# Weight maxima turned by TensorE, the last 42 MLP rows stacked, and sums of rotated terms moved to VectorE

## The chip, the cores and the metric

One core of one Trainium2 chip. The metric is the device time of one execution in microseconds, as the median of several runs. Lower is better.

## The reference, cut to what matters

The input is x of 4 x 2048 x 256 in float32. Every step works on the layer norm of what came before, and its own layer norm is added to x.

```python
x = x + layernorm(self_attention(layernorm(x)))      # scores x @ x.T, softmax over axis 1, whole sequence
y = layernorm(x)
for l in range(2):                                   # DEPTH = 2
    q, k, v = split(shift_token(y) @ wqkv[l])        # 8 heads of 64
    q, k = l2norm(q) * q_scale, l2norm(k) * k_scale  # then rotated: t * cos + rotate_half(t) * sin
    y = y + local_attention(q, k, v) @ wo[l]         # windows of 128, each with the window before it
    h = layernorm(shift_token(y)) * ln_g[l] + ln_b[l]
    a, g = split(h @ w1[l] + b1[l])                  # HID = 682 each = 5 * 128 + 42
    y = y + (a * gelu(g)) @ w2[l] + b2[l]
out = x + layernorm(y)
```

## The kernel before, in words

The work is cut in windows of 128 rows: 64 of them (4 sequences of 16), and as each passes two layers, 128 steps in the second part. Five queues run side by side and meet at semaphores: SP issues all DMAs, PE is TensorE, DVE is VectorE, ACT is ScalarE, POOL is GpSimd. Each engine does its instructions strictly in the order written; an order across engines exists only where one waits.

**Phase A** is the attention over whole sequences. For each sequence TensorE makes 16 blocks of scores, then 16 windows of context, called products (line 657): 48 matmuls of 256 columns per window, into PSUM banks 0 to 3 in turn. VectorE closes each window in finish(g) (lines 512 to 546): statistics of the product (L519 to L523), normalising it (L529), adding the input (L533, x_res, loaded two windows ahead), statistics of the sum (L535 to L539), normalising that (L546). It needs two inverse roots in between, and both come from GpSimd: rstd_c (L349, L351) before L529 and rstd_x (L355) before L546. SP stores both results. TensorE may be at most three windows ahead of L529.

In the last sequence, the scratch memory of the scores is free again, and the weights of the MLP are loaded there by early_weights() (lines 257 to 268: w1, w2, then wo). They must be scaled by powers of two before they are split in two float16 halves. For this, VectorE takes maxima of |w2| in windows 4 and 5 and of |w1| in windows 6 to 9 (L465, L471); tops(), after window 10, brings them to one value per partition for three quantities and two layers, and a square for each layer (L477 to L483). share_tops() on GpSimd, after window 10, takes the maximum over the 128 partitions of the six columns and the sum over the partitions of the two squares, with two partition_all_reduce (L319, L321). scales(), on VectorE after window 13, waits for both and makes the factors, 15 small instructions in a chain (L488 to L510).

**Phase B** begins behind a barrier of all engines. Weights are split in halves by ScalarE (L779 to L789) and VectorE (L794 to L813), and then a software pipeline runs over 128 slots (plus 6 to drain). In slot s:
- TensorE turns q and k of window s-1 (L994, L1001), projects window s (L1016, 18 matmuls of 512 columns), turns the probabilities of s-2 (L1032), multiplies them with v (L1044), makes the scores of s-1 (L1057), multiplies the attention's output of s-2 with wo (L1070), and turns the input of s+1 (L983). In an even slot it then makes the first product of the MLP for a pair of windows (L1091, 66 matmuls), in an odd slot the second (L1103).
- ScalarE squares q and k for the norms, copies from PSUM, and does the exponentials and the gelu.
- VectorE makes the two terms of the rotation of q and k (L1216, L1217: t1 and t2), sums the squares (L1224), adds the context in an odd slot of layer 1 (L1266, fin + x2), takes the low half of the attention output (L1271), reduces eight heads of scores (L1303), then the residual (L1324), normalises probabilities (L1315, eight times), takes the low half of the next input (L1203) and, in an even slot, finishes the MLP's hidden chunks (L1337, six of them).
- GpSimd halves the squares (L1380), in an odd slot splits hidden chunks 4 and 5 in halves (L1352, L1354; chunks 0 to 3 at the end of an even slot), adds t1 and t2 for q (L1388, qr) and for k (L1390, kr_sum), clamps the sums of squares (L1394), takes the inverse root for k (L1396), multiplies k with it (L1400, kr), and takes the inverse root for q (L1404). TensorE's L994 needs qr and its L1001 needs kr.

Products of float32 accuracy are made of high and low halves: PARTS = ((0, 0), (0, 1), (1, 0)) is high by high, high by low, low by high. L1103 runs over n in 2 windows, 6 chunks of the hidden rows and these three parts, 36 matmuls of 256 columns; chunk 5 (FULL) holds 42 rows (REST), the other partitions being zero.

## Time and profile before

| | |
|---|---|
| median of 3 runs | 3042.15 us (3039.99 to 3045.44) |
| the profiled execution's own time | 3045.73 us |
| its span, first to last instruction | 3043.9 us |
| TensorE | 2896.4 us busy, 95%, 25720 matmuls, clock granted 0.982 of full on average |
| VectorE | 2421.9 us, 80% |
| ScalarE | 2044.8 us, 67% |
| GpSimd | 2045.6 us, 67% |
| DMA | 179.01 MB, mean 59 GB/s |

All numbers below are from this one profiled execution, and so are to be set against 3045.73 us. A timeline row gives the start and the length of an instruction (or of a run of equal ones, with their count), the engine, the line of the kernel, what is written and what is read, and in brackets how long the engine was idle just before and what ended that. Lengths of neighbours on VectorE overlap by some 0.1 us, so that the distance of starts is the better price. Phase A and its load of weights take up to about 691 us; the stream of phase B begins at about 713 us.

### The profile page before, as it was taken

The page shows a single profiled execution, that of the slowest core. Times are in us where ns is not written, and L with a number is a line of the kernel's source. Part 1 is how long each engine was busy: PE and PEld are TensorE (multiplying, and loading weights), DVE is VectorE, ACT ScalarE, POOL GpSimd, SP SyncE. Part 2 cuts the span into 40 slices and gives each one's busy share as a digit, 9 for nine tenths or more (in the row PEclk, how much of TensorE's full clock was granted, in tenths as well). Part 3 has the DMA queues.
Part 4 walks back from the last instruction along what each step waited for, and adds up shares of the span by engine and source line. Part 5 has one row for each costly group of instructions (what it writes and reads, how often), then busy time and mean ns, then how long its engine had stood idle before and what let it go on. Part 6 is the DMA issues. An engine that isn't in the chain of part 4 may idle for free. (4 is left out here: it accounts for less than half of the span.)

```text
span 3043.9 us, 81674 instructions
## 1 busy us (share of the span) xinstructions
PE 2896.4 (95%) x25720; PEld 2508.8 (82%) x25720; DVE 2421.9 (80%) x6767; ACT 2044.8 (67%) x4648; POOL 2045.6 (67%) x2782
## 2 busy tenths in 40 slices
PE   7899999984999999999999999999999999999996
PEld 4767777773888888888888888888888888888885
DVE  7779898756778778777777877788888888888884
ACT  6234343504777777777777777777788787778874
POOL 0432323014777777777777777888888888888884
PEclk9999999987999999999999999999999999999998
DMA  1421212212111121111111111122222112222221
GB/s 40 143 83 39 74 35 70 91 55 75 53 50 50 52 58 50 54 50 48 51 54 55 50 55 50 50 59 61 66 57 62 55 55 59 64 61 59 60 53 44
DMA packets 274932, 179.01 MB, mean 59 GB/s; under 512 B 96014, under 2 KB 271090, under 8 KB 274802
## 3 DMA queue, kind: packets, MB, share of 16 engines
q1 hardware_dynamic: 274802, 177.34, 20.1%
q8 instruction: 75, 1.23, 0.2%
q14 instruction: 55, 0.45, 0.1%
HBM read 105.92 MB, written 54.54 MB: 53 GB/s over the span
## 5 line engine op out<-in xcount | busy, mean ns | idle before, releaser
L1177 ACT ACTIVATE b_front<-b_front,b_negmax 128x256 f32<-128x256 f32 x1024 | 507.8, 497 | 77.2 <-DVE b_negmax L1303 76.4
L1016 PE MATMUL b_ps<-b_wqkv,b_hT_hi 128*128 128x512 f32 x1536 | 497.1, 405 | 2.6 <-issue 1.5
L1091 PE MATMUL b_ps<-b_h2T,b_w 128*128 128x256 f16 x4224 | 474.2, 273 | 9.2 <-DMA b_h2T<-b_xh_hl 9.2
L1091 PEld LDWEIGHTS b_ps<-b_h2T,b_w 128*128 128x128 f16 x4224 | 414.2, 98 | 58.3 <-DMA b_h2T<-b_xh_hl 8.8
L1315 DVE TENSOR_SCALAR b_front<-b_front,b_rinv 128x256 f32<-128x256 f32 x1024 | 338.4, 393 | 9.1
L1016 PEld LDWEIGHTS b_ps<-b_wqkv,b_hT_hi 128*128 128x128 f32 x1536 | 283.1, 191 | 61.4 <-issue 2.2
L1303 DVE CUSTOM_DVE_ANT_0 b_front<-b_ps,b_mask,b_rn 128x256 f32<-128x256 f32 x768 | 317.7, 479 | 0.0
L1159 ACT COPY b_front<-b_ps 128x512 f32<-128x512 f32 x512 | 260.8, 593 | 80.3 <-PE b_ps L1032 80.3
L1016 PE MATMUL b_ps<-b_wqkv,b_hT_lo 128*128 128x512 f32 x768 | 305.9, 398 | 0.0
L1271 DVE TENSOR_TENSOR b_oT<-b_ps,b_oT 128x512 fp32r<-128x512 f32 x128 | 88.6, 692 | 262.6 <-ACT b_oT L1168 262.6
L1354 POOL TENSOR_TENSOR b_hid_hl<-b_front,b_hid_hl 128x256 f16<-128x256 f32 (+1 forms) x384 | 258.7, 674 | 31.0
L1103 PE MATMUL b_ps<-b_w,b_hid_hl 128*128 128x256 f16 x2304 | 264.8, 274 | 3.3 <-POOL b_hid_hl L1354 3.3
L1044 PE MATMUL b_ps<-b_front 128*64 128x128 f32 x4096 | 253.0, 276 | 0.9 <-ACT b_front L1159 0.9
L1103 PEld LDWEIGHTS b_ps<-b_w,b_hid_hl 128*128 128x128 f16 x2304 | 226.5, 98 | 30.4 <-POOL b_hid_hl L1354 3.6
L1032 PEld LDWEIGHTS b_ps<-b_ident_f,b_front 128*128 128x128 f32 x2048 | 232.1, 141 | 22.0 <-DVE b_xpp L1247 3.3
L1032 PE MATMUL b_ps<-b_ident_f,b_front 128*128 128x128 f32 x2048 | 245.4, 273 | 4.3 <-DVE b_xpp L1247 3.1
L1044 PEld LDWEIGHTS b_ps<-b_front 128*64 128x64 f32 x4096 | 221.5, 137 | 23.5 <-issue 13.5
L1352 POOL CAST b_hid_hl<-b_front 128x256 f16<-128x256 f32 (+1 forms) x384 | 165.2, 430 | 111.2 <-DVE b_front L1337 92.8
L1192 ACT ACTIVATE b_gl<-b_ps,b_b,b_w_unit 128x256 f32<-128x256 f32 (+1 forms) x384 | 202.9, 561 | 54.7 <-PE b_ps L1091 32.4
L1337 DVE SCALAR_TENSOR_TENSOR b_front<-b_ps,b_b1a,b_gl 128x256 f32<-128x256 f32 (+1 forms) x384 | 177.4, 480 | 62.8 <-ACT b_gl L1192 60.9
L1404 POOL TENSOR_TENSOR b_rn<-b_ss_min,b_mhalf 128x8 f32<-128x8 f32 x128 | 223.4, 1745 | 0.0
L1396 POOL TENSOR_TENSOR b_rn_k<-b_ss_min,b_mhalf 128x8 f32<-128x8 f32 x128 | 214.0, 1672 | 10.7
(171 smaller groups left out, 7076.0 us busy)
## 6 DMA issues: line engine op xcount, KB each, us to landing
b_hx<-xs_dram SPq DMA_DIRECT2D x256, 64.0 KB, 1.9
b_rot<-rot_dram SPq DMA_DIRECT2D x128, 128.0 KB, 2.1
b_xr<-xs_dram SPq DMA_DIRECT2D x128, 128.0 KB, 2.1
xp_dram<-b_xp SPq DMA_DIRECT2D x128, 128.0 KB, 1.7
b_h<-xp_dram SPq DMA_DIRECT2D x256, 64.0 KB, 1.8
a_x_res<-in_L_attn_x_dram SPq DMA_DIRECT2D x64, 128.0 KB, 2.2
x_dram<-a_x SPq DMA_DIRECT2D x64, 128.0 KB, 1.7
xs_dram<-a_xo SPq DMA_DIRECT2D x64, 128.0 KB, 1.8
```

The source lines that it names most:

```text
L1016: last = nc.tensor.matmul(ps[:, bank, :], hT[:, k, :], wqkv[:, ds(layer(s), 1), part, k, bank * INNER:(bank + 1) * INNER], start=(k == 0 a ...
L1032: last = nc.tensor.transpose(ps[:, 3 + p, n * P:(n + 1) * P], probs[:, 2 * p + n // 2, (n % 2) * P:(n % 2 + 1) * P], ident_f[:])
L1044: last = nc.tensor.matmul(ps[h * DH:(h + 1) * DH, 7, p * P:(p + 1) * P], v[:, window, (2 * p + h) * DH:(2 * p + h + 1) * DH], probsT[:, p, ...
L1091: last = nc.tensor.matmul(ps[:, bank, half * 2 * P:(half + 1) * 2 * P], w1[:, ds(layer(2 * j), 1), wp, k, first:first + P], h2T[:, hp, k, ...
L1103: last = nc.tensor.matmul(ps[:, 3, n * D:(n + 1) * D], hid_hl[:, hp, c, n * P:(n + 1) * P], w2[:, ds(layer(2 * j), 1), wp, c, :], start=(c ...
L1159: nc.scalar.copy(probsT[:, p, :], ps[:, 3 + p, :]).then_inc(pT_kept, 1)
L1177: nc.scalar.activation(probs[:, h, :], probs[:, h, :], ACT.Exp, bias=negmax[:, h:h + 1], scale=-1.0, accum_out=rowsum[:, h:h + 1]).then_in ...
L1303: nc.vector.tensor_tensor_reduce(probs[:, h, :], head_scores(h), which, rn[:, (r - 1) % 2, h:h + 1], ABOVE_ALL, ALU.add, ALU.min, negmax[: ...
L1315: nc.vector.tensor_scalar(probs[:, h, :], probs[:, h, :], rinv[:, h:h + 1], None, ALU.mult).then_inc(probs_ready, 1)
L1354: nc.gpsimd.tensor_tensor(hid_hl[rows, 1, c, :], hid[rows, c, :], hid_hl[rows, 0, c, :], ALU.subtract).then_inc(hid_lo, 1)
L1396: nc.gpsimd.tensor_tensor(rn_k[:], ss_min[:, HEADS:2 * HEADS], mhalf[:, 0:HEADS], ALU.pow).then_inc(rnk_ready, 1)
L1404: nc.gpsimd.tensor_tensor(rn[:, r % 2, :], ss_min[:, 0:HEADS], mhalf[:, 0:HEADS], ALU.pow).then_inc(rn_ready, 1)
```

## The change

1. share_tops() leaves GpSimd. tops() stays after window 10. TensorE turns the six columns after product 12 (turn_tops, into PSUM bank 7), VectorE reduces them over the columns to six values and spreads these on a diagonal after window 12 (highest_tops), and TensorE multiplies a matrix of ones with the diagonal and with the squares after product 14 (share_tops, bank 6). scales() moves from after window 13 to after window 14, and begins with two copies out of PSUM. GpSimd clears a 128x128 matrix of ones at the start.
2. Chunk 5 of the hidden rows: its low half is written to partitions 64 to 105 of the high half's tile, w2's last 42 rows are loaded twice (partitions 0 to 41 and 64 to 105), and L1103 makes two parts instead of three there. GpSimd waits for its last write of a pair. The loads of w2 and wo count on one semaphore, and the maxima of w2 wait for all six.
3. A function sum_terms on VectorE stands between sum_squares and add_context. It makes k's sum of t1 and t2 in odd slots, and q's and k's in slots 0 to 3 (filling(s) is true there alone). GpSimd makes the others: q's from slot 4 on, k's in even slots from 4 on.

```diff
+REST_PARTS = ((0, 0), (0, 1))
-W2_MAXIMA_AT, W1_MAXIMA_AT, SHARE_AT, SCALES_AT = 4, 6, 10, 13
+W2_MAXIMA_AT, W1_MAXIMA_AT, TOPS_AT, TURN_AT, SCALES_AT = 4, 6, 10, 12, 14
...
@@ early_weights(), SP @@
-                sp.dma_start(early.w2_f[0:REST, :, FULL, :], w["w2"][:, FULL * P:HID, :].rearrange("l p d -> p l d")).then_inc(early.loaded_w2, 16)
+                for first_row in (0, SECOND_REST):
+                    sp.dma_start(early.w2_f[first_row:first_row + REST, :, FULL, :], w["w2"][:, FULL * P:HID, :].rearrange("l p d -> p l d")).then_inc(early.loaded_w2, 16)
...
@@ phase A, POOL @@
+            nc.gpsimd.memset(ones[:], 1.0).then_inc(pool_consts, 1)
...
-            def share_tops():
-                pool.wait_ge(early.top_ready, 3)
-                nc.gpsimd.partition_all_reduce(early.top_all[:].rearrange("p n l -> p (n l)"), early.top[:].rearrange("p n l -> p (n l)"), P,
-                                               RED_MAX).then_inc(early.top_shared, 1)
-                nc.gpsimd.partition_all_reduce(early.sq_all[:], early.top_sq[:], P, RED_ADD).then_inc(early.top_shared, 1)
...
-                    if g == NW - WPB + SHARE_AT:
-                        share_tops()
...
@@ weight_maximum(), DVE @@
-                    dve.wait_ge(early.loaded_w2, 16 * 3)
+                    dve.wait_ge(early.loaded_w2, 16 * (4 + LAYERS))
...
+            def highest_tops():
+
+                dve.wait_ge(early.top_turned, 1)
+                nc.vector.tensor_reduce(highest[:], ps[0:by_weight, 7, 0:P], AX.X, ALU.max).then_inc(early.tops, 1)
+                dve.wait_ge(early.tops, 3)
+                nc.vector.tensor_scalar(spread[:], ident_f[0:by_weight, 0:by_weight], highest[:], None, ALU.mult).then_inc(early.top_ready, 1)
...
             def scales():
                 dve.wait_ge(early.top_shared, 2)
+                nc.vector.tensor_copy(top_all[:].rearrange("p n l -> p (n l)"), ps[:, 6, 0:by_weight]).then_inc(early.tops, 1)
+                nc.vector.tensor_copy(early.sq_all[:], ps[:, 6, by_weight:by_weight + LAYERS]).then_inc(early.tops, 1)
+                dve.wait_ge(early.tops, 5)
...
@@ phase A, PE @@
+                def turn_tops():
+
+                    pe.wait_ge(early.top_ready, 3)
+                    nc.tensor.transpose(ps[0:by_weight, 7, 0:P], early.top[:].rearrange("p n l -> p (n l)"), ident_f[:]).then_inc(early.top_turned, 1)
+
+                def share_tops():
+
+                    pe.wait_ge(pool_consts, 2)
+                    pe.wait_ge(early.top_ready, 4)
+                    nc.tensor.matmul(ps[:, 6, 0:by_weight], ones[0:by_weight, :], spread[:], start=True, stop=True).then_inc(early.top_shared, 1)
+                    nc.tensor.matmul(ps[:, 6, by_weight:by_weight + LAYERS], ones[:], early.top_sq[:], start=True, stop=True).then_inc(early.top_shared, 1)
...
@@ phase B, L1103, PE @@
-                                for a, (hp, wp) in enumerate(PARTS):
+                                for a, (hp, wp) in enumerate(PARTS if c < FULL else REST_PARTS):
...
@@ phase B, DVE @@
+                def sum_terms(s, r):
+
+                    if filling(s):
+                        dve.wait_ge(q_terms, 2 * (s + 1))
+                        wait(dve, qT_done, s)
+                        nc.vector.tensor_tensor(qr[:], t1[:, 0, :], t2[:, 0, :], ALU.add).then_inc(qr_ready, 1)
+                    if in_range(s) and (filling(s) or r % 2 == 1):
+                        dve.wait_ge(k_terms, 2 * (s + 1))
+                        nc.vector.tensor_tensor(t1[:, 1, :], t1[:, 1, :], t2[:, 1, :], ALU.add).then_inc(kr_sum, 1)
...
                     sum_squares(s)
+                    sum_terms(s, r)
                     add_context(pairs - 3, r, layer)
...
@@ phase B, hid_halves(), POOL @@
-                            nc.gpsimd.tensor_tensor(hid_hl[rows, 1, c, :], hid[rows, c, :], hid_hl[rows, 0, c, :], ALU.subtract).then_inc(hid_lo, 1)
+                            low = hid_hl[rows, 1, c, :] if c < FULL else hid_hl[SECOND_REST:SECOND_REST + REST, 0, c, :]
+                            nc.gpsimd.tensor_tensor(low, hid[rows, c, :], hid_hl[rows, 0, c, :], ALU.subtract).then_inc(hid_lo, 1)
+                            if c == FULL:
+                                pool.wait_ge(hid_lo, HC * (j + 1))
...
@@ phase B, run(), POOL @@
-                    if in_range(s):
+                    if in_range(s) and not filling(s):
                         pool.wait_ge(q_terms, 2 * (s + 1))
                         wait(pool, qT_done, s)
                         nc.gpsimd.tensor_tensor(qr[:], t1[:, 0, :], t2[:, 0, :], ALU.add).then_inc(qr_ready, 1)
+                    if in_range(s) and not filling(s) and r % 2 == 0:
                         pool.wait_ge(k_terms, 2 * (s + 1))
                         nc.gpsimd.tensor_tensor(t1[:, 1, :], t1[:, 1, :], t2[:, 1, :], ALU.add).then_inc(kr_sum, 1)
```

## Rows read from the trace of the kernel before

**Rows 1.** Busy us (x count) by stretch: PE, PEld, DVE, ACT, POOL, clock, DMA
```profile
900.00:1500.00 600.00, 600.00 (x5525) 535.81 (x5523) 473.16 (x1422) 458.70 (x1120) 474.31 (x621) 1.00 0.18 52
...
2000.00:2500.00 500.00, 499.48 (x4591) 445.60 (x4589) 425.50 (x1252) 398.39 (x959) 429.55 (x573) 1.00 0.21 60
```
**Rows 2.** PE timeline, seam: start, length, what, xcount, [idle before <-what ended it]
```profile
624.78 46.56 PE L657 MATMUL a_ps<-a_xn_odd,a_E 128*128 128x256 f16 x425
```
**Rows 3.** Timeline of DVE at the seam
```profile
645.17 0.43 DVE L519 BATCH_NORM_STATS2 a_st_c<-a_ps 128x6 f32<-128x256 f32 x1 [0.50 <-PE a_ps L657]
...
650.41 0.43 DVE L519 BATCH_NORM_STATS2 a_st_c<-a_ps 128x6 f32<-128x256 f32 x1
...
664.57 0.54 DVE L529 TENSOR_SCALAR a_ln_c<-a_ps,a_mv_c,a_rstd_c 128x256 f32<-128x256 f32 x1 [13.32 <-POOL a_rstd_c L351]
...
676.68 0.15 DVE L488 TENSOR_TENSOR b_bias_sq<-b_top_all 128x2 f32<-128x2 f32 x1
...
678.69 0.16 DVE L510 TENSOR_TENSOR b_w_unit<-b_w1a_unit,b_w_low 128x2 f32<-128x2 f32 x1
...
683.39 0.42 DVE L519 BATCH_NORM_STATS2 a_st_c<-a_ps 128x6 f32<-128x256 f32 x1
...
687.68 0.42 DVE L546 TENSOR_SCALAR a_xo<-a_x,a_mv_x,a_rstd_x 128x256 f32<-128x256 f32 x1 [0.66 <-POOL a_rstd_x L355]
```
**Rows 4.** Timeline of POOL at the seam
```profile
655.22 0.40 POOL L319 PARTITION_ALL_REDUCE b_top_all<-b_top  x1 [5.80 <-issue]
...
663.68 0.59 POOL L349 TENSOR_TENSOR a_pow_c<-a_var_c,a_mhalf 128x1 f32<-128x1 f32 x1 [7.67 <-issue]
```
**Rows 5.** Timeline of PE in the first slots of phase B
```profile
730.58 1.11 PE L1001 MATMUL b_ps<-b_ident_f,b_kr 128*128 128x128 f32 x4 [3.85 <-POOL b_kr L1400]
...
743.89 1.17 PE L1016 MATMUL b_ps<-b_wqkv,b_hT_hi 128*128 128x512 f32 x2
```
**Rows 6.** Timeline of PE in the stream, layer 0, then layer 1
```profile
1233.54 4.09 PE L1103 MATMUL b_ps<-b_w,b_hid_hl 128*128 128x256 f16 x36
...
1237.47 0.60 PE L994 MATMUL b_ps<-b_ident_f,b_front 128*128 128x128 f32 x4
...
2225.00 1.69 PE L1070 MATMUL b_ps<-b_wo,b_oT 128*128 128x256 f32 x12
```
**Rows 7.** Timeline of POOL in slots 0 and 1
```profile
725.98 1.26 POOL L1390 TENSOR_TENSOR b_front<-b_front 128x512 f32<-128x512 f32 x1
...
729.48 1.04 POOL L1400 TENSOR_TENSOR b_kr<-b_front,b_rn_k 128x512 f32<-128x512 f32 x1
...
742.00 1.04 POOL L1400 TENSOR_TENSOR b_kr<-b_front,b_rn_k 128x512 f32<-128x512 f32 x1
```
**Rows 8.** DVE timeline, an odd slot of layer 0, then of layer 1
```profile
1230.93 0.69 DVE L1271 TENSOR_TENSOR b_oT<-b_ps,b_oT 128x512 fp32r<-128x512 f32 x1 [2.65 <-ACT b_oT L1168]
...
2221.36 1.00 DVE L1266 TENSOR_TENSOR b_fin<-b_fin,b_x 128x512 f32<-128x512 f32 x1
...
2224.13 0.69 DVE L1271 TENSOR_TENSOR b_oT<-b_ps,b_oT 128x512 fp32r<-128x512 f32 x1 [1.76 <-ACT b_oT L1168]
```
**Rows 9.** The line L1266: ns min/median/max, first and last start
```profile
L1266 DVE TENSOR_TENSOR b_fin<-b_fin,b_x x32: 693/1006/1197, 1972.6 to 3040.4; 128x512 f32<-128x512 f32 x32
```
**Rows 10.** Timeline of DVE in slots 1 and 2
```profile
741.52 1.93 DVE L1315 TENSOR_SCALAR b_front<-b_front,b_rinv 128x256 f32<-128x256 f32 x4
...
743.37 0.41 DVE L1203 TENSOR_TENSOR b_hT_lo<-b_ps,b_hT_hi 128x256 fp32r<-128x256 f32 x1
...
743.90 1.14 DVE L1315 TENSOR_SCALAR b_front<-b_front,b_rinv 128x256 f32<-128x256 f32 x4
...
754.18 0.69 DVE L1271 TENSOR_TENSOR b_oT<-b_ps,b_oT 128x512 fp32r<-128x512 f32 x1 [2.98 <-ACT b_oT L1168]
```
**Rows 11.** Timeline of SP, the issue of the last w2 load
```profile
585.48 0.92 SPq L266 DMA_DIRECT2D b_front<-in_L_ffn_w_dram  x1
```
**Rows 12.** Timeline of DVE, window 6 of the last batch
```profile
624.21 0.43 DVE L519 BATCH_NORM_STATS2 a_st_c<-a_ps 128x6 f32<-128x256 f32 x1 [8.55 <-PE a_ps L657]
```

More of the change, by code:

```diff
@@ L126, in __init__ @@
         self.w1_unit, self.w2_unit = sb("w1_unit", [P, LAYERS]), sb("w2_unit", [P, LAYERS])
-        self.cleared, self.loaded_bias, self.loaded_w2, self.loaded_wo = (sem(n) for n in (
-            "cleared", "loaded_bias", "loaded_w2", "loaded_wo"))
+        self.cleared, self.loaded_bias, self.loaded_w2 = (sem(n) for n in (
+            "cleared", "loaded_bias", "loaded_w2"))
         self.loaded_w1 = [sem(f"loaded_w1_{l}") for l in range(LAYERS)]
-        self.bias_done, self.w1_gained, self.maxima, self.tops, self.top_ready, self.top_shared = (sem(n) for n in (
-            "bias_done", "w1_gained", "maxima", "tops", "top_ready", "top_shared"))
+        self.bias_done, self.w1_gained, self.maxima, self.tops, self.top_ready, self.top_shared, self.top_turned = (sem(n) for n in (
+            "bias_done", "w1_gained", "maxima", "tops", "top_ready", "top_shared", "top_turned"))
         self.step, self.scale_ready = sem("step"), sem("scale_ready")
@@ L179, in phase_a @@
         zeros = sb("zeros", [LAYERS * B, D])
+        ones = sb("ones", [P, P])
+        by_weight = 3 * LAYERS
+        highest, spread = sb("highest", [by_weight, 1]), sb("spread", [by_weight, by_weight])
         ps = ctx.enter_context(nc.psum_tensor("a_ps", [P, 8, 512], F32))
@@ L220, in _ @@
                 sp.dma_start(x_ring[:, n % ring, :], x_v[:, n, :]).then_inc(ring_in[n % ring], 16)
-            sp.wait_ge(pool_consts, 1)
+            sp.wait_ge(pool_consts, 2)
             rows = BLOCKS_PER_BATCH * P
@@ L556, in _ @@
                     finish(g)
-                    if g == NW - WPB + SHARE_AT:
+                    if g == NW - WPB + TOPS_AT:
                         tops()
+                    if g == NW - WPB + TURN_AT:
+                        highest_tops()
                     if g == NW - WPB + SCALES_AT:
@@ L690, in _ @@
                         biases(i - W2_MAXIMA_AT)
+                    elif i == TURN_AT:
+                        turn_tops()
+                    elif i == SCALES_AT:
+                        share_tops()
                 if b < B - 1:
@@ L697, in in_range, with filling @@
     return not isinstance(t, int) or 0 <= t < NT
+def filling(s):
+    return isinstance(s, int) and s < SLOTS
 def slots(eng, run):
@@ L776, in _ @@
             def _(act):
-                act.wait_ge(early.loaded_wo, 16 * LAYERS)
+                act.wait_ge(early.loaded_w2, 16 * (4 + LAYERS))
                 for l in range(LAYERS):
@@ L1101, in run @@
                             for c in range(HC):
-                                for a, (hp, wp) in enumerate(PARTS):
+                                for a, (hp, wp) in enumerate(PARTS if c < FULL else REST_PARTS):
                                     last = nc.tensor.matmul(ps[:, 3, n * D:(n + 1) * D], hid_hl[:, hp, c, n * P:(n + 1) * P],
                                                             w2[:, ds(layer(2 * j), 1), wp, c, :],
-                                                            start=(c == 0 and a == 0), stop=(c == HC - 1 and a == 2))
+                                                            start=(c == 0 and a == 0), stop=(c == HC - 1 and a == 1))
                         last.then_inc(w2_done, 1)
@@ L1432, in _ @@
                 nc.gpsimd.memset(kT_low[:].bitcast(F32), 0.0).then_inc(vk_cleared, 1)
-                nc.gpsimd.memset(hid_hl[:, :, FULL, :], 0.0).then_inc(vk_cleared, 1)
+                nc.gpsimd.memset(hid_hl[:, 0, FULL, :], 0.0).then_inc(vk_cleared, 1)
                 slots(pool, run)
```

4 lines of the change are left out of this document (2 added, 2 removed).

## The prediction

> **What bounds the kernel now.** I read the busy time by stretches first [rows 1]. In the stream of slots that fills the last three quarters of the span, TensorE is busy for 600.00 of 600 us in one stretch and 499.48 of 500 in the other, at the full clock; VectorE and GpSimd have some 15 to 20% free. There a microsecond off TensorE's queue is a microsecond off the end, and one moved between VectorE and GpSimd is worth nothing unless it makes TensorE wait. The seam between the phases is another matter: TensorE does its last product of phase A at 624.78 + 46.56 = 671.34 [rows 2], but VectorE closes the last window only at 687.68 + 0.42 = 688.10 [rows 3], and phase B waits for that. So at the seam VectorE's chain is the path, and it was held: L529 stood 13.32 us for GpSimd [rows 3], whose queue had the two all-reduces of share_tops ahead of that window's root, with 5.80 and 7.67 us of idle around them [rows 4]. The 0.40 us shown for an all-reduce is no measure of it, the 13.32 is. Last, in the first slots of phase B TensorE waits for GpSimd's k, 3.85 us at L1001 [rows 5].
>
> **The change, part by part.**
>
> (a) The seam. Two all-reduces leave GpSimd. TensorE gains a transpose after product 12 and two matmuls of 6 and 2 columns after product 14; VectorE gains a reduction and a 6x6 scaling after window 12, and two small copies ahead of the scale chain, which moves from behind window 13 to behind window 14. Without the stall each window is closed as its product comes: products come 650.41 - 645.17 = 5.24 us apart, closing one takes 683.39 to 688.10, 4.71 us [rows 3]. Window 11 starts at 650.41 as before, 12 at 655.65, closed at 660.36. Now the reduction and the scaling: the transpose they wait for is in TensorE's queue at 655.65 and done by 656. I give both, with their waits, 0.55 us (small instructions here take 0.15, and the 15 of the scale chain, many of which wait for the one before, run from 676.68 to 678.85 [rows 3]); they end at 660.9. Window 13 starts at 655.65 + 5.24 + 0.3 = 661.2, so they are hidden; the 0.3 is the transpose, as four of 128x128 took 1.11 us after an idle [rows 5]. Window 14 starts at 666.4 and is closed at 671.1. TensorE's two matmuls stand at 666.4 and want VectorE's 660.9: 5.5 us of room. Then the scale chain, 678.69 + 0.16 - 676.68 = 2.17 us, with two copies and a wait, 0.4: 673.7. Window 15, its product done by 671.9, ends at 673.7 + 4.71 = 678.4. Against 688.10 that is **-9.7 us**. Bounds: with all seven new instructions free, 650.41 + 3 x 5.24 + 4.71 + 2.17 + 4.71 = 677.7, -10.4; with 0.15 us more for each, -8.6. All of phase B starts behind this barrier and shifts with it.
>
> (b) The sixth chunk of the MLP's second product. Per pair of windows 36 matmuls of 256 columns become 34. The 36 take from 1233.54 to 1237.47, 3.93 us, 0.109 each [rows 6]. 64 pairs make 128 fewer: **-13.9 us**. Bounds: -13.5 if the last two pairs, where TensorE may wait anyway, give nothing; -14.2 if one is spared at half the clock. GpSimd's last subtraction writes other partitions at its old size, and GpSimd then waits for its own write, some 0.1 us per pair. Queued behind that wait are q's sum and the norms; k's own sum leaves that queue, so all of it still ends earlier than now.
>
> (c) Odd slots, k's sum on VectorE. GpSimd loses one instruction of 1.26 us [rows 7] in each of 64 slots; VectorE gains one of about 0.69, the length of L1271, which also has 512 columns [rows 8]. It stands after the sum of squares and ahead of L1271, before which VectorE idles 2.65 us in layer 0 and 1.76 in layer 1 [rows 8]. So it costs nothing, and the relief of GpSimd brings nothing, as TensorE waits for neither. Layer 1 needs a closer look, as L1266 stands in the same gap and reads both operands from the same memory, as the new sum does. L1266 takes 1.006 us by the median and 0.693 at least [rows 9]: beside a busy GpSimd such an instruction is held up. I give the sum L1266's place and length, 2221.36 to 2222.36, and L1266 another 1.0 behind it, to 2223.4. ScalarE's input for L1271 comes at 2224.13 [rows 8], 0.7 later. Still nothing, with less room. Without that cover each 0.1 us would count, as L1271 ends at 2224.82 and TensorE's L1070, which needs it, starts at 2225.00 [rows 6].
> The Trainium skill (SBUF — State Buffer, "Who interferes with whom") has a rule for this: a VectorE instruction with two inputs in SBUF and a GpSimd instruction that reads SBUF exclude each other, and the later one waits for the whole of the earlier. The spread of L1266 from 0.693 to 1.197 us agrees. By it the sum could stand behind a whole GpSimd sum, and the rival below comes of that; GpSimd would be held as well.
>
> (d) Slots 0 to 3, both sums on VectorE. In slot 0 two sums of 1.26 us leave GpSimd's queue between the halving and the norms. VectorE's sum of squares, also over 512 columns, is ready a 0.69 and a wait after the halving, some 0.8 us, so the norms start 2 x 1.26 - 0.8 = 1.7 us earlier, and k is out 1.7 us before its 729.48 + 1.04 = 730.52 [rows 7]; 0.8 if VectorE's sums and the norms' first steps hold each other up. In slot 1 VectorE is the path: L1203 ends at 743.37 + 0.41 = 743.78 [rows 10] and TensorE's projections start at 743.89 [rows 5]. The new sums put 2 x 0.6 us ahead of it. Against that VectorE starts 0.8 to 1.7 earlier, and four L1315 that took 1.93 us beside GpSimd's L1400 at 742.00 [rows 7, 10] take 1.14, as the next four do, once L1400 is done earlier. Middle of the bounds: -1.25 - 0.8 + 1.2, **-0.9 us**, from -0.4 to -1.3. In slots 2 and 3 the 1.2 us fall into an idle of 2.98 before L1271 [rows 10]: nothing. The outermost bounds are -1.7 (only k's chain counts) and +1.2 (only VectorE's queue).
>
> (e) Costed at nothing: one more load for w2, 84 KB. SP's issue of the one like it took 0.92 us [rows 11], so the loads, stores and residual rows behind it come up to that much later, and so does the closing of window 3; VectorE's 8.55 us of idle at 624.21 [rows 12] cover it, without them it would be 0.9. W2's maxima now wait for wo's loads too, in front of the same cover. The memset of the ones stands where GpSimd waits for the first rows.
>
> **Sum.** -9.7 - 13.9 - 0.9 = -24.5 us. The profiled execution took 3045.73 us (3043.9 of span and 1.8 around it); one like it would take 3021.2. It lies 3.6 above the median of the three runs, 3042.15; from the median the sum gives 3017.7.
>
> **Rivals.**
> The two engines lock each other out (slower). In layer 1's odd slots L1266 loses to GpSimd's last subtraction and then to q's sum of 1.26 us as well, and ends some 1.8 us later than I gave, at 2225.2. L1271 then starts 1.07 late, and TensorE at L1070 with it. 29 slots (the 32 of L1266 less three after the last projections) by 1.07 is +31: 3048.7. It decides once L1266 ends past 2224.13. For it: the mere 0.2 us of room between L1271 and L1070. Against: L1266 never took over 1.197 us [rows 9]. 0.04.
> The shorter product is absorbed. TensorE is at the next slot 0.22 us sooner and waits there for VectorE's L1203 or GpSimd's k. Then (b) gives nothing: 3031.6. Against: TensorE has no idle in 600 us [rows 1]. 0.07.
> The seam gives half: TensorE's in-order queue stands at one of its two new waits, or the barrier is held by something that the stall hid. 3022.6. The 5.5 us of room speak against it. 0.08.
> The edits do not do what they say, or two of these together: 3036 and above. 0.03.
>
> **How the numbers follow.** The forecast keeps 0.78; its own range, with its bounds and the 3 us by which runs of a kernel lie from the median, is 3012 to 3023. To hold 8 in 10 with something for what no row shows, I go on to the second rival: 3010 to 3031. A measurement can tell some 0.2%, 6 us, from no change. Faster 0.78 + 0.07 + 0.08 = 0.93, within 0.2% 0.03, slower 0.04.
>
> **What would show it.** (a) No wait of L529 over 1 us; the last window closed near 678.4. (b) L1103 x2176, 34 matmuls in 3.71 us, two slots 0.22 us shorter. (c) VectorE's sum 0.7 us long, up to 1.2 beside GpSimd; L1070 with no idle. (d) k 0.8 to 1.7 us earlier in slot 0, slot 2's projections 0.9 earlier, both counted from the barrier. The prediction would be wrong if TensorE showed waits at L1070 in layer 1, or if the time from its last product of phase A to its first work in phase B stayed what it was.

## The result, and the profile after

| | before | changed |
|---|---|---|
| median of the runs on one chip | 3043.80 us (3039.99 to 3046.31) | **3021.36 us** (3019.62 to 3025.50) |
| ratio, 95% interval | | **0.9929** [0.9915, 0.9942] |
| profiled execution, span | 3043.9 us | 3023.7 us |

The kernel is 0.7% faster, 22.4 us by the medians and 20.2 by the spans of the two profiled executions. First the page's busy times, as in the table ahead of the prediction.

```profile
PE 2887.6 (95%) x25597; PEld 2497.1 (83%) x25597; DVE 2466.3 (82%) x6841; ACT 2043.6 (68%) x4648; POOL 1978.3 (65%) x2711
```

GpSimd has lost 67 us of work (2045.6 before), VectorE has gained 44. Of each, what matters is where. In the rows that follow, lines have moved: L519, L529, L546 and L657 of phase A are L527, L537, L554 and L667 now, and L994, L1016, L1032, L1070, L1103, L1266 and L1271 of phase B are L1025, L1047, L1063, L1101, L1134, L1307 and L1312.

**The seam**, from the timeline of all engines, against [rows 3]:

```profile
655.77 0.27 PE L685 MATMUL a_ps<-a_ident_f,b_top 128*6 128x128 f32 x1
...
657.73 0.54 DVE L537 TENSOR_SCALAR a_ln_c<-a_ps,a_mv_c,a_rstd_c 128x256 f32<-128x256 f32 x1 [0.92 <-POOL a_rstd_c L351]
...
660.59 0.27 DVE L486 TENSOR_REDUCE a_highest<-a_ps 6x1 f32<-6x128 f32 x1
660.89 0.22 DVE L488 TENSOR_SCALAR a_spread<-a_ident_f,a_highest 6x6 f32<-6x6 f32 x1
661.33 0.43 DVE L527 BATCH_NORM_STATS2 a_st_c<-a_ps 128x6 f32<-128x256 f32 x1 [0.21 <-PE a_ps L667]
...
666.46 0.38 PE L691 MATMUL a_ps<-a_spread,a_ones 6*128 6x6 f32 x2
...
671.18 0.16 DVE L493 COPY b_top_all<-a_ps 128x6 f32<-128x6 f32 x1
...
673.53 0.42 DVE L527 BATCH_NORM_STATS2 a_st_c<-a_ps 128x6 f32<-128x256 f32 x1
...
677.81 0.41 DVE L554 TENSOR_SCALAR a_xo<-a_x,a_mv_x,a_rstd_x 128x256 f32<-128x256 f32 x1 [0.66 <-POOL a_rstd_x L355]
...
681.11 0.37 DVE L825 TENSOR_SCALAR b_b1a<-b_b,b_w1a_scale 128x6 f32<-128x6 f32 x2 [2.89 <-PEq L149]
```

The wait of 13.32 us before L529 is 0.92 now, as for every other window. TensorE's ones product stands 5.4 us behind the 6x6 scaling that it needs and waits for nothing. The last window is closed at 677.81 + 0.41 = 678.22, where it was 688.10, and phase B's first work after the barrier starts at 681.11, 9.87 us sooner than before:

```profile
690.98 0.36 DVE L794 TENSOR_SCALAR b_b1a<-b_b,b_w1a_scale 128x6 f32<-128x6 f32 x2 [2.88 <-PEq L148]
```

**The stream.** One pair of slots takes 35.253 us where it took 35.420. This is the distance from the first L1134 of one pair to that of the next, as a mean of 24 pairs in the steady part of a layer, which is 12 rounds of the loop of four slots; both layers give the same. That is 0.167 less, not the 0.218 that two matmuls cost. The timeline of TensorE after, layer 0, and under it the same two steps before:

```profile
1220.79 3.88 PE L1134 MATMUL b_ps<-b_w,b_hid_hl 128*128 128x256 f16 x34
1224.50 0.60 PE L1025 MATMUL b_ps<-b_ident_f,b_front 128*128 128x128 f32 x4
...
1225.29 0.71 PE L1047 MATMUL b_ps<-b_wqkv,b_hT_hi 128*128 128x512 f32 x2
...
1229.58 1.91 PE L1063 MATMUL b_ps<-b_ident_f,b_front 128*128 128x128 f32 x16
```

```profile
1238.26 0.71 PE L1016 MATMUL b_ps<-b_wqkv,b_hT_hi 128*128 128x512 f32 x2
...
1242.52 1.91 PE L1032 MATMUL b_ps<-b_ident_f,b_front 128*128 128x128 f32 x16
```

The 34 matmuls take 1224.50 - 1220.79 = 3.71 us, as forecast. But the 18 projection matmuls of a slot, between the first L1047 and L1063, take 4.29 us where they took 4.26; in the steady part of layer 0 it is 4.289 in every slot, against 4.264 in even and 4.275 in odd ones. Nothing in the change touches them. With some 0.01 us elsewhere that is 0.05 us per pair taken back.

**The odd slot of layer 1**, where the lock was feared [rows 8], from the timeline after:

```profile
2204.59 1.01 DVE L1259 TENSOR_TENSOR b_front<-b_front 128x512 f32<-128x512 f32 x1
2205.52 0.88 DVE L1307 TENSOR_TENSOR b_fin<-b_fin,b_x 128x512 f32<-128x512 f32 x1
...
2205.93 0.99 POOL L1397 TENSOR_TENSOR b_hid_hl<-b_front,b_hid_hl 42x256 f16<-42x256 f32 x1
...
2207.15 1.29 POOL L1433 TENSOR_TENSOR b_front<-b_front 128x512 f32<-128x512 f32 x1 [0.23 <-POOL b_hid_hl L1397]
...
2207.36 0.69 DVE L1312 TENSOR_TENSOR b_oT<-b_ps,b_oT 128x512 fp32r<-128x512 f32 x1 [0.96 <-ACT b_oT L1199]
...
2208.22 1.69 PE L1101 MATMUL b_ps<-b_wo,b_oT 128*128 128x256 f32 x12
```

The new sum takes 1.01 us, L1307 0.88 behind it, and L1312 still waits 0.96 us for ScalarE: TensorE's L1101 loses nothing. GpSimd's last subtraction pays, 0.99 us for 0.67, and its wait for its own write costs it 0.23 more.

### The profile page after: what moved, and what is told of

It is laid out like the page before. It is cut to its first block and busy times, and to the rows that moved or that the text cites. A ratio compares the mean times of both kernels' runs of the same rounds, so it can differ in the third digit from the quotient of the medians.

```text
span 3023.7 us, 81512 instructions
## 1 busy us (share of the span) xinstructions
PE 2887.6 (95%) x25597; PEld 2497.1 (83%) x25597; DVE 2466.3 (82%) x6841; ACT 2043.6 (68%) x4648; POOL 1978.3 (65%) x2711
## 3 DMA queue, kind: packets, MB, share of 16 engines
q1 hardware_dynamic: 274900, 177.42, 20.2%
## 5 line engine op out<-in xcount | busy, mean ns | idle before, releaser
L1047 PE MATMUL b_ps<-b_wqkv,b_hT_hi 128*128 128x512 f32 x1536 | 497.9, 405 | 2.9 <-issue 1.9
L1047 PEld LDWEIGHTS b_ps<-b_wqkv,b_hT_hi 128*128 128x128 f32 x1536 | 282.6, 191 | 63.4 <-issue 2.7
L1357 DVE TENSOR_SCALAR b_front<-b_front,b_rinv 128x256 f32<-128x256 f32 x1024 | 324.4, 379 | 9.0
L1047 PE MATMUL b_ps<-b_wqkv,b_hT_lo 128*128 128x512 f32 x768 | 306.9, 400 | 0.0
L1397 POOL TENSOR_TENSOR b_hid_hl<-b_front,b_hid_hl 128x256 f16<-128x256 f32 (+1 forms) x384 | 268.7, 700 | 31.0
L1312 DVE TENSOR_TENSOR b_oT<-b_ps,b_oT 128x512 fp32r<-128x512 f32 x128 | 88.5, 691 | 208.1 <-ACT b_oT L1199 208.1
L1394 POOL CAST b_hid_hl<-b_front 128x256 f16<-128x256 f32 (+1 forms) x384 | 180.9, 471 | 114.5 <-DVE b_front L1379 95.5
L1134 PE MATMUL b_ps<-b_w,b_hid_hl 128*128 128x256 f16 x2176 | 250.9, 274 | 3.3 <-POOL b_hid_hl L1397 3.3
L1063 PEld LDWEIGHTS b_ps<-b_ident_f,b_front 128*128 128x128 f32 x2048 | 232.7, 141 | 24.8 <-DVE b_xpp L1288 4.7
L1063 PE MATMUL b_ps<-b_ident_f,b_front 128*128 128x128 f32 x2048 | 246.0, 274 | 5.4 <-DVE b_xpp L1288 4.1
L1134 PEld LDWEIGHTS b_ps<-b_w,b_hid_hl 128*128 128x128 f16 x2176 | 214.2, 99 | 28.9 <-POOL b_hid_hl L1397 3.6
L1442 POOL TENSOR_TENSOR b_rn_k<-b_ss_min,b_mhalf 128x8 f32<-128x8 f32 x128 | 215.0, 1680 | 10.7
L1101 PE MATMUL b_ps<-b_wo,b_oT 128*128 128x256 f32 x1536 | 216.2, 290 | 1.4 <-DVE b_oT L1312 1.4
```

Source lines behind the costliest of these rows:

```text
L1047: last = nc.tensor.matmul(ps[:, bank, :], hT[:, k, :], wqkv[:, ds(layer(s), 1), part, k, bank * INNER:(bank + 1) * INNER], start=(k == 0 a ...
L1063: last = nc.tensor.transpose(ps[:, 3 + p, n * P:(n + 1) * P], probs[:, 2 * p + n // 2, (n % 2) * P:(n % 2 + 1) * P], ident_f[:])
L1101: last = nc.tensor.matmul(ps[:, 2, 0:D], oT[:, op, p, :], wo[:, ds(layer(t), 1), wp, p, :], start=(p == 0 and a == 0), stop=(p == HP - 1 a ...
L1134: last = nc.tensor.matmul(ps[:, 3, n * D:(n + 1) * D], hid_hl[:, hp, c, n * P:(n + 1) * P], w2[:, ds(layer(2 * j), 1), wp, c, :], start=(c ...
L1357: nc.vector.tensor_scalar(probs[:, h, :], probs[:, h, :], rinv[:, h:h + 1], None, ALU.mult).then_inc(probs_ready, 1)
L1397: nc.gpsimd.tensor_tensor(low, hid[rows, c, :], hid_hl[rows, 0, c, :], ALU.subtract).then_inc(hid_lo, 1)
```

## The experiments

**1. The parts alone.** Each of the first three kernels is the kernel before with one part of the change; the fourth leaves one piece out of the changed kernel. A ratio is against the kernel before, timed beside the run (medians of 3043.6 to 3044.5 us).

seam_only: the constants, turn_tops, highest_tops, share_tops on TensorE, and scales behind window 14.

```diff
-W2_MAXIMA_AT, W1_MAXIMA_AT, SHARE_AT, SCALES_AT = 4, 6, 10, 13
+W2_MAXIMA_AT, W1_MAXIMA_AT, TOPS_AT, TURN_AT, SCALES_AT = 4, 6, 10, 12, 14
```

> Only the weight maxima go through TensorE; the second MLP product and the sums are as before. Theory (the seam is VectorE's chain, held by the all-reduces): the last window of phase A is closed 9.9 us earlier, the time falls by 9 to 11 us, and the distance from slot to slot in phase B is unchanged: 35.42 us per pair of slots. Rival (half of the gain was a shift by something else): 5 us or less.

Measured: 3033.39 us (3030.67 to 3034.22), ratio 0.9962 [0.9949, 0.9976]. In the trace TensorE's product with wo stands 11.2 us sooner from window 8 through layer 0 and 11.0 through layer 1: a shift that phase B hardly changes. The pair stays at 35.42 us and the projections at 4.264 and 4.275. (a) is what it was said to be, within what one execution can show: here the barrier came 11.5 us sooner, in the changed kernel's trace 9.9, and TensorE's last product of phase A ended at 670.82 here and at 672.41 there.

w2_only: the stacking, 34 matmuls, GpSimd's own wait.

```diff
-                                for a, (hp, wp) in enumerate(PARTS):
+                                for a, (hp, wp) in enumerate(PARTS if c < FULL else REST_PARTS):
```

> Only the last 42 rows stacked: 34 instead of 36 matmuls per pair. In the changed kernel a pair of slots became 0.167 us shorter where 2 x 0.109 = 0.218 was taken off; the 18 projection matmuls took 4.289 us in every slot, against 4.264 and 4.275 before. Theory A (VectorE's new sum in odd slots costs TensorE these 0.05 us): here 35.20 us per pair and 13.5 us less in all. Theory B (it comes with the shorter program of TensorE itself or with the stacking): 35.25 us per pair, projections 4.289 us, 10 us less in all.

Measured: 3040.28 us (3037.65 to 3044.51), ratio 0.9989 [0.9980, 0.9998], 4 us where 13.9 were removed; neither theory foresaw it. In layer 0 the pair is 35.253 us and TensorE is 7.6 us ahead by window 61, of which 2.7 stood there already at window 2, before the stream. In layer 1 the pair is 35.520, longer than before, and 2.3 of the 7.6 are given back by window 120, 3.3 with the last windows. So (b) does not pay by itself in layer 1.

sums_only: sum_terms on VectorE, in odd slots and in slots 0 to 3.

```diff
+                    if in_range(s) and (filling(s) or r % 2 == 1):
+                        dve.wait_ge(k_terms, 2 * (s + 1))
+                        nc.vector.tensor_tensor(t1[:, 1, :], t1[:, 1, :], t2[:, 1, :], ALU.add).then_inc(kr_sum, 1)
```

> Only the sums of rotated terms on VectorE (k's in odd slots, both in the first four). Theory A: the projections take 4.289 us in every slot and a pair 35.47 us, so 3 us are lost over the stream and about 1 won in the first slots: 0 to 3 us slower. Theory B: projections as before, 35.42 us per pair, only the first slots gain: 1 us faster. The forecast of the prediction is the latter.

Measured: 3040.32 us (3037.70 to 3048.39), ratio 0.9991 [0.9982, 1.0000]; in its trace TensorE is 0.2 us ahead of the kernel before in layer 0 and 0.5 behind in layer 1, so that the 4 us between the medians are not found in the trace. The pair is 35.42 and the projections are 4.264 and 4.275: the sums have nothing to do with the 0.05 us.

odd_on_pool: the changed kernel with k's sum of odd slots back on GpSimd.

```diff
-                    if in_range(s) and (filling(s) or r % 2 == 1):
+                    if in_range(s) and filling(s):
```

> The changed kernel with k's sum of the odd slots back on GpSimd (those of the first four slots stay on VectorE). Theory A: 35.20 us per pair, 3 us faster than the changed kernel. Theory B: 35.25 us per pair, the same time as the changed kernel within 1 us.

Measured: 3031.68 us (3030.02 to 3032.34), ratio 0.9959 [0.9945, 0.9972]: **10.3 us slower than the changed kernel** by the medians, 9.1 by the ratios, where both theories had it as fast or faster. In layer 0 the pair is 35.253 either way; in layer 1 it is 35.50 against 35.253. In the traces TensorE's product with wo stands 0.4 us later than the changed kernel's at window 61, 6.9 at window 122 and 8.3 at the last. So k's odd sum, worth nothing alone, is what makes (b)'s gain collectible in layer 1. How, the timelines show. L1315 (the normalisations), L1400 (GpSimd's product for k) and L1044 (TensorE's product with the probabilities) are L1356, L1445 and L1074 in w2_only, and one line further in the changed kernel. First w2_only, layer 1, an odd slot and the even one behind it:

```profile
2216.34 1.30 POOL L1432 TENSOR_TENSOR b_front<-b_front 128x512 f32<-128x512 f32 x1 [0.23 <-POOL b_hid_hl L1396]
...
2219.47 3.88 PE L1133 MATMUL b_ps<-b_w,b_hid_hl 128*128 128x256 f16 x34
...
2221.07 1.04 POOL L1445 TENSOR_TENSOR b_kr<-b_front,b_rn_k 128x512 f32<-128x512 f32 x1
2221.24 1.81 DVE L1356 TENSOR_SCALAR b_front<-b_front,b_rinv 128x256 f32<-128x256 f32 x4
...
2224.81 0.74 POOL L1456 TENSOR_TENSOR b_front<-b_xp,b_b 128x256 f32<-128x256 f32 x1 [0.91 <-DVE b_front L1356]
2225.51 0.69 POOL L1405 TENSOR_TENSOR b_xh_hl<-b_xh,b_xh_hl 128x256 f16<-128x256 f32 x1
...
2226.72 1.21 SPq L954 DMA_TRANSPOSE b_h2T<-b_xh_hl  x1
...
2229.23 0.60 ACT L1162 ACTIVATE b_xh_hl<-b_h,b_shift,b_rstd 128x256 f16<-128x256 f32 x1 [0.51 <-DMA b_h2T<-b_xh_hl]
2229.74 2.03 ACT L1189 COPY b_front<-b_ps 128x512 f32<-128x512 f32 x4
...
2230.36 2.12 PE L1074 MATMUL b_ps<-b_front 128*64 128x128 f32 x32 [0.19 <-ACT b_front L1189]
```

And the changed kernel, the same steps:

```profile
2209.97 3.88 PE L1134 MATMUL b_ps<-b_w,b_hid_hl 128*128 128x256 f16 x34
...
2210.63 1.04 POOL L1446 TENSOR_TENSOR b_kr<-b_front,b_rn_k 128x512 f32<-128x512 f32 x1
...
2211.74 1.14 DVE L1357 TENSOR_SCALAR b_front<-b_front,b_rinv 128x256 f32<-128x256 f32 x4
...
2214.64 0.74 POOL L1457 TENSOR_TENSOR b_front<-b_xp,b_b 128x256 f32<-128x256 f32 x1 [1.37 <-DVE b_front L1357]
2215.33 0.68 POOL L1406 TENSOR_TENSOR b_xh_hl<-b_xh,b_xh_hl 128x256 f16<-128x256 f32 x1
...
2216.53 1.21 SPq L955 DMA_TRANSPOSE b_h2T<-b_xh_hl  x1
...
2219.08 0.59 ACT L1163 ACTIVATE b_xh_hl<-b_h,b_shift,b_rstd 128x256 f16<-128x256 f32 x1
2219.57 2.02 ACT L1190 COPY b_front<-b_ps 128x512 f32<-128x512 f32 x4
```

Starts counted from the first matmul of the second product, means over the 24 pairs of layer 1, in us:

| | w2_only | before | changed |
|---|---|---|---|
| GpSimd, product for k | 1.62 | 1.33 | 0.67 |
| VectorE, first four normalisations | 1.77 | 1.77 | 1.77 |
| the same, how long they take | 1.82 | 1.54 | 1.14 |
| GpSimd, low half of the MLP's input | 6.01 | 5.72 | 5.32 |
| SP, transposed load of it | 7.10 | 6.81 | 6.41 |
| ScalarE, first copy of the probabilities | 10.13 | 9.93 | 9.65 |
| pair of slots | 35.520 | 35.420 | 35.253 |

VectorE's normalisations start at the same moment in all three. In w2_only they meet GpSimd's product and take 1.81 us for 1.14 (the two fences); that is the stretching of [rows 10], four L1315 beside L1400. The kernel before has it too (1.54), and there it costs nothing: in sums_only it is gone, they take 1.14, and the pair stays at 35.42. In layer 0 w2_only's product starts at 1.12 and the four take 1.33, and its pair is the changed kernel's. What is behind the normalisations shifts, and TensorE's product with the probabilities waits for ScalarE's copies (the row with 0.19). So the chain is read as GpSimd, VectorE, GpSimd, SP, DMA, ScalarE, TensorE, and only its last link shows as TensorE's wait (7 times in 500 us of layer 1, once in a round of two pairs).

**2. GpSimd's own wait.** w2_unstacked_34 writes the last chunk's low part where it used to be, and makes no product of it.

```diff
-                            low = hid_hl[rows, 1, c, :] if c < FULL else hid_hl[SECOND_REST:SECOND_REST + REST, 0, c, :]
+                            low = hid_hl[rows, 1, c, :]
...
-                            if c == FULL:
-                                pool.wait_ge(hid_lo, HC * (j + 1))
```

> w2_only without the stacking: the last chunk's low part goes to its old place, GpSimd's wait for its own write is gone, and 34 matmuls are made. The product of that low part (42 rows) with w2's high part is left out of the output. Theory A (what w2_only lost in layer 1 is GpSimd's queue, 0.23 to 0.27 us later for that wait): pair of slots 35.25 us in both layers, GpSimd's k starts within 0.1 us of where it did in the kernel before plus 0.17, time 3031 to 3035. Theory B (the wait hardly matters; TensorE, 0.17 us sooner, runs into the same chain whatever is there): pair in layer 1 at 35.42 or above, where the chain of GpSimd sets it, time 3036 to 3040. In both, TensorE's 18 projection matmuls tell whether stacking has to do with their 4.289 us: 4.289 here as well acquits it, 4.264 and 4.275 would convict it.

Measured: 3033.89 us (3033.03 to 3037.69), ratio 0.9965 [0.9951, 0.9978], 6.4 us faster than w2_only. Pair 35.253 in layer 0 and 35.307 in layer 1, k's product at 1.33 again and the four normalisations at 1.54. So the wait of 0.23 us, which holds up all that is behind it in GpSimd's queue, costs 0.213 of the 0.267 us that a pair of w2_only loses in layer 1. The rest, 0.054, fits TensorE coming sooner to a chain that is where it was. The time is Theory A's, the pair a little above it. The projections take 4.289 in layer 0 here too, so stacking is not their cause.

**3. The lock.** both_odd_on_dve gives VectorE q's sum in odd slots too.

```diff
-                    if filling(s):
+                    if in_range(s) and (filling(s) or r % 2 == 1):
                         dve.wait_ge(q_terms, 2 * (s + 1))
```

> The changed kernel with q's sum of the odd slots on VectorE too. This puts the prediction's first rival to the test: VectorE has about 1 us between its residual sum and oT's low part in layer 1's odd slots. Theory A (a sum beside GpSimd takes 0.7 to 1.0 us and just fits): oT's low part starts at most 0.1 us later, GpSimd's queue is 1.2 us earlier and nobody collects it, time within 3 us of the changed kernel, 3018 to 3024. Rival (the lock): the sums and the residual sum take 1.0 each, oT's low part starts 0.3 to 1.0 us late in 29 slots of layer 1 and TensorE waits for it at wo: 9 to 29 us, 3030 to 3050.

Measured: 3040.11 us (3037.11 to 3042.74), ratio 0.9984 [0.9975, 0.9993], 18.7 us slower than the changed kernel. The time is the rival's, the place is not. The two sums and L1307 take 1.01, 0.88 and 1.15 us and use up the whole gap: L1312 stands right behind them, with no wait left.

```profile
2209.30 1.01 DVE L1256 TENSOR_TENSOR b_front<-b_front 128x512 f32<-128x512 f32 x1
2210.23 0.88 DVE L1259 TENSOR_TENSOR b_front<-b_front 128x512 f32<-128x512 f32 x1
2211.03 1.15 DVE L1307 TENSOR_TENSOR b_fin<-b_fin,b_x 128x512 f32<-128x512 f32 x1
2212.11 0.68 DVE L1312 TENSOR_TENSOR b_oT<-b_ps,b_oT 128x512 fp32r<-128x512 f32 x1
```

But counted from ScalarE's copy, which it needs, L1312 starts only 0.05 us later than in the changed kernel, and L1101 comes on time. The pair is 35.253 in layer 0 and 35.909 in layer 1, where pairs of 35.25 and some 36.6 us alternate, and VectorE's waits of 300 us of layer 1 name another place: four times, once in each round of the loop of four slots, it idles 1.95 us in the mean ahead of its first instruction of the round, with nothing awaited (total, times, longest).

```profile
DVE b_qT_low L1320 <- issue: 7.8, 4, 2.2
```

The DMA view of the same 300 us has a queue that the changed kernel does not show there (packets, MB, share):

```profile
q14 instruction: 20, 0.16, 0.2%
```

**4. Where a loop lies.** Both kernels add nothing but waits for a semaphore that has long been reached (two of them make one instruction of the built program), at VectorE's start of phase B, where it is idle: both_odd_shift_36 to both_odd_on_dve, with N = 72, and shift_20 to the changed kernel, with N = 40.

```diff
+                for _ in range(N):
+                    dve.wait_ge(early.tops, 5)
                 keep_hT(0)
                 slots(dve, run)
```

> The kernel both_odd_on_dve with 36 instructions more on VectorE ahead of its loops: waits for a semaphore that has long been reached, at the start of phase B, where VectorE has nothing to do. What both_odd_on_dve lost shows in its trace as 1.95 us of idle before VectorE's first instruction of each round of layer 1's loop (four slots), with nothing awaited, and the DMA view has 44 packets of instructions (0.36 MB) in 600 us of layer 1 where the changed kernel has at most 2. Theory P (position: VectorE's loop of layer 1, 292 instructions long, starts at its instruction 2483, where its end no longer stands in store together with its start, so the round's start is fetched anew each time; the changed kernel's, 288 long from 2467, just stands): 36 further on it stands again. No such idle, no packets of instructions in the loop, pair of slots 35.25 us in both layers, time within 3 us of the changed kernel, 3018 to 3025. Theory L (load: two sums on VectorE in odd slots are too much for it or lock it against GpSimd, and the idle is a wait that the profile does not name): all stays as it was, pair 35.83 us in layer 1, 3037 to 3043. The Trainium skill (Runtime: NRT & Kernel Launch, Instruction fetch mechanics) says that the store holds two blocks of 256 instructions and that a branch to one outside of them waits for a fetch; by that the loop stands if it crosses one block boundary and not if it crosses two.

> The changed kernel with 20 of the same waits ahead of VectorE's loops and nothing else: its layer 1 loop, 288 long, starts at instruction 2487 in place of 2467. Theory P: by the positions of both_odd_on_dve (2483, does not stand) and the changed kernel (2467, stands) it no longer stands. VectorE idles some 1.9 us at the start of each round of layer 1's loop, packets of instructions appear (some 40 in 600 us), pair 35.75 to 35.90 us in layer 1 and 35.25 in layer 0, time 14 to 19 us over the changed kernel, 3035 to 3041. Theory L: 20 idle waits at a place where VectorE has nothing to do cost nothing, 3019 to 3025.

Measured: both_odd_shift_36 3022.71 us (3021.24 to 3025.06), ratio 0.9928 [0.9915, 0.9942], pair 35.253 in both layers, no such idle, no packets of instructions in layer 1's loop. shift_20 3038.64 us (3035.46 to 3039.39), ratio 0.9979 [0.9970, 0.9988], pair 35.253 in layer 0 and 35.909 in layer 1 (the 35.90 of the expectation is just passed), 44 packets in 600 us of layer 1 (2100 to 2700). both_odd_on_dve has 44 in the same stretch, and no other kernel here has any, so that w2_only and odd_on_pool owe nothing to it. VectorE's waits of shift_20, and its DMA view of those 600 us:

```profile
DVE b_qT_low L1320 <- issue: 8.2, 4, 2.2
```

```profile
q14 instruction: 44, 0.36, 0.2%
```

Theory P holds both ways: 36 idle instructions win 17.4 us, 20 of the same lose 17.3. And the lock rival falls: with both sums on VectorE and the loop in place, the time is that of the changed kernel within 1.4 us. It falls narrowly, as the two sums leave nothing of the gap before L1312; a third sum there was not tried.

**5. The first slots.** fill_on_pool: filling() is false everywhere. By this edit k's sums of slots 1 and 3 stay on VectorE (its trace has slot 1's there, 1.15 us long at 727.35), which the expectation has otherwise.

```diff
-    return isinstance(s, int) and s < SLOTS
+    return False
```

> The changed kernel with both sums of slots 0 to 3 back on GpSimd (k's odd sums stay on VectorE in all later slots and go back in these four). Theory: slot 0's k comes 1.7 to 2.3 us later counted from the barrier, slot 2's projections 0.7 to 0.9 us later, and the stream keeps that 0.9 us to the end, with the same 35.25 us per pair: 3022 to 3026 for one run. Rival: the filling is set by VectorE's rotation and the sums' place is worth under 0.2 us.

Measured: 3026.11 us in one run. GpSimd's product for k of slot 0 starts 38.52 us behind the barrier where the changed kernel has 36.24 (2.28 later, as expected). The stream is 0.82 us later than the changed kernel's from window 8 through layer 0 and 0.88 at the last product with wo. But in this execution the barrier came 2.1 us sooner, at 678.98, and TensorE's granted clock was 0.50 in both traces up to 710 us, though slot 0's projections had begun at 705.37 here and at 707.49 there. So counted from the barrier slot 2 lies 2.3 us later (54.47 for 52.18), and counted from the rise of the clock (710.79 and 710.36) it lies 0.3 us sooner. The 0.8 is of the expected size, and it is not a clean measure of the sums.

**6. What takes the 0.05 us back.** The changed kernel with other numbers of matmuls: 36 (the old third part, now zeros, is multiplied again), 35 (for one window alone), 32 (the last rows' product with w2's low part is left out).

```diff
-                                for a, (hp, wp) in enumerate(PARTS if c < FULL else REST_PARTS):
+                                for a, (hp, wp) in enumerate(PARTS):
```

> The changed kernel with the two matmuls put back (the last chunk's low part of old, now all zeros, by w2's high part, which adds nothing): 36 matmuls, stacking and all else kept. Rows of all kernels so far: the 18 projection matmuls take 4.289 us with 34 matmuls in the second MLP product and 4.264 (even slot) and 4.275 (odd) with 36. Theory A (it is the number of TensorE's instructions in the loop, not the stacking nor GpSimd's write): the projections go back to 4.264 and 4.275, pair 35.42 us, time 10.7 us over the changed kernel, 3031 to 3034. Theory B (the stacking or the moved write does it): they stay at 4.289, pair 35.47 us, time 14 us over it, 3034 to 3038.

> As stacked_36, with the extra matmul for the first of the two windows alone: 35. Second product 3.82 us. Theory A1 (the projections' time follows how TensorE's program lies, in no order with its length): anything from 4.25 to 4.31. Theory A2 (TensorE gives back a share of what is left out, about 0.025 us per projection group and matmul pair saved): halfway, 4.276 and 4.282, pair 35.34.

> The changed kernel with two more matmuls left out (the last chunk's product with w2's low part, for both windows): 32. The product of the last 42 rows with w2's low part is missing from the output, and so is the low part of the hidden values there. Second product 3.49 us. Theory A1: the projections anywhere from 4.25 to 4.31. Theory A2: twice the loss, 4.31 in both slots, pair 35.09. Where TensorE is 0.17 us earlier still, layer 1 may show the next wait: without one the pair is the same in both layers.

| matmuls | time, us | pair of slots, us | projections, even / odd slot, us |
|---|---|---|---|
| 36 (before) | 3043.80 | 35.420 | 4.264 / 4.275 |
| 36, stacked | 3031.71 (3030.09 to 3035.20) | 35.420 | 4.264 / 4.275 |
| 35, stacked | 3029.53 (one run) | 35.313 | 4.269 / 4.275 |
| 34 (changed) | 3021.36 | 35.253 | 4.289 / 4.289 |
| 32, stacked | 3007.09 (one run) | 35.007 | 4.261 / 4.289 |

stacked_36 has the ratio 0.9968 [0.9956, 0.9980] and is 10.4 us over the changed kernel: the two matmuls are worth 0.167 x 64 = 10.7, not 13.9. The projections change with the number of matmuls made elsewhere on TensorE, and in no order: their even slots take 4.264, 4.269, 4.289 and 4.261 us for 36, 35, 34 and 32. Theory A2, a share given back, falls with the last. Single steps from matmul to matmul are irregular with 36 (228 to 241 ns) and alternate with 34 (229, 238). Why is open. That TensorE's loop of one layer lies elsewhere in its program than that of the other speaks against its position, as the projections are the same in both layers.

## Why the prediction was right, and where not

The forecast was 3017.7 us, in a range of 3010 to 3031, with 0.93 for faster; 3021.36 was measured. Against the sum:

| step | predicted | measured |
|---|---|---|
| (a) seam | -9.7 | -9.9 (barrier to barrier) |
| (b) matmuls | -13.9 | -10.7 |
| (d) first slots | -0.9 | -0.9 (L1101 of windows 2 and 3: 10.81 sooner, less 9.87), in these two executions |
| (c), (e) | 0 | 0 by themselves |
| crossing from layer 0 to 1 | none | +0.7 |
| last windows and the end | none | +0.3 |
| sum | -24.5 | -20.5 (spans: -20.2) |

(a) is right step by step: 678.22 for the 678.4 given, the reduction and the scaling hidden in the gap, and no more wait than the 0.92 us of every window. Here the seam's chain could be read in full before.

(b) The price of the 34 is right to 0.01 us. The term was too large by 3.2 us because the engine's other work was taken as fixed: "a microsecond off TensorE's queue is a microsecond off the end" holds for what is taken off, but what stays is not of fixed length when the stream around it changes.

(c) **The step that was wrong** is "the relief of GpSimd brings nothing, as TensorE waits for neither". It is right of the kernel before, as sums_only shows, and wrong of the kernel that (b) makes. What it left out is that an instruction of GpSimd can end up beside VectorE's normalisations and make them longer. TensorE 0.17 us sooner per pair and GpSimd 0.29 later (1.33 to 1.62), 0.23 of it by the wait that was put at 0.1, are enough for the chain from k's product to ScalarE's copies to come out last. Part (b) also says "all of it still ends earlier than now": true, since k's product went from 1.33 to 0.67, and it is what the gain of layer 1 hangs on. The prediction had the link in its hand: in (d) it priced L1315 beside L1400, and did not ask where else the two meet. So "the shorter product is absorbed" (0.07) is real when (c) is missing, in another chain than the one named; with (c) it did not happen.

To that extent the range held by luck. Of the 22 us, 8 to 10 hang on a piece that the prediction priced at nothing; without it (odd_on_pool) the median is 3031.68, just outside the range that was stated.

Sum on VectorE: 1.00 given for layer 1, 1.01 measured; L1307 behind it 0.88, for 1.0. The rule of the Trainium skill cited then (SBUF — State Buffer, "Who interferes with whom": a two-input instruction of VectorE and GpSimd's reads exclude each other) agrees: 1.01 us beside GpSimd for the 0.69 of L1312 with one operand in PSUM, and GpSimd's subtraction 0.99 for 0.67. The lock, the rival drawn from it, did not come, because the gap was wide enough: L1312 keeps 0.96 us of wait in layer 1. A second sum uses all of it up and makes L1312 0.05 us late, which TensorE does not feel.

(d) can't be confirmed to the size given. GpSimd's product for k of slot 0 starts 2.25 us earlier, counted from the barrier, where k was to be 0.8 to 1.7 earlier, and slot 2's projections 0.72 earlier, for 0.9. But by L1101 of windows 2 and 3, sums_only, which has the same first slots, gains 0.2 us over its barrier and odd_on_pool 0.3, while w2_only, which has not, gains 0.4: executions differ by more than the term. (e) shows no cost: the idle that was to cover it [rows 12] is 8.56 us for 8.55.

Not foreseen and not followed further are two losses. At the crossing of the layers (windows 60 to 78) TensorE gains 0.85 us where nine pairs would give 1.50. From window 118 to the last it loses 0.4 where 0.75 were to be gained; there it waits 3.9 us for VectorE's xpp where it waited 3.1. After its last product with wo 0.85 us come back.

That no loop was fetched anew was luck. The change adds 4 instructions to VectorE's loop of layer 1 and moves it by 25, counted in the built programs. It now starts at instruction 2467 and has 288; 20 further on, 17 of the 22 us are gone, as shift_20 shows. The Trainium skill (Runtime: NRT & Kernel Launch, Instruction fetch mechanics) has it that an engine's store keeps two blocks of 256 instructions and that a branch to outside of them waits for a fetch. An estimate from that page's block size: the four positions agree with it if 42 to 61 entries stand ahead of the program's first instruction, which no run here shows. Then 2467 with 288 and 2519 with 292 touch two blocks, 2483 with 292 and 2487 with 288 touch three, and the changed kernel has room for 19 instructions at most. That position alone switches the packets and the 1.95 us per round is shown, by 36 instructions that take them away and 20 that bring them; the number of blocks is the Trainium skill's.

## What to carry to other kernels

An instruction taken off an engine that nobody waits for can still decide what another saving is worth: look at the chain that comes out second once a saving is made, and take parts out of the whole as well as testing them alone (k's odd sum showed nothing in its trace alone, and 8 to 10 us in company). Look for where two engines' instructions already stretch each other (here a mean length that mixes 1.14 us with 1.54 or 1.93), as a shift of 0.3 us moves such a meeting in or out. And when a kernel with a hardware loop loses time that no wait explains, look at the engine's first instruction of each round for idle under "issue", and at the DMA view for instruction packets, before blaming the edit: moving the loop by some idle instructions tells the two apart.

## What the hardware showed that was not expected

- A round of VectorE's loop that is fetched anew idles 1.95 us in the mean (2.05 in shift_20), 2.2 at most, and costs TensorE 1.31 us per round of four slots (2 x (35.909 - 35.253)), 17 us in all; 5 packets and 43 KB per round (44 packets and 0.36 MB in 600 us).
- The same 18 matmuls take between 4.261 and 4.289 us, by how many matmuls the stream has elsewhere.
- Four normalisations of VectorE with one operand in SBUF take 1.82 us where GpSimd's product of 1.04 starts 0.15 us before them, 1.54 where it starts 0.44 before, and 1.14 free of it. The power of 1.7 us (L1450), which GpSimd runs beside them in the changed kernel, does not stretch them.
- A GpSimd instruction that waits for GpSimd's own last write starts 0.23 us after that ended.
